# Unread matmuls in idle steps, feed-forward matmuls in halves, and own placing tables for the ends of a chunked recurrence

## The chip, the cores and the metric

The kernel runs on one core of a Trainium2 chip. The metric is the device time of one execution in microseconds (us).

## What is computed

An RWKV-7 block is followed by a routed feed-forward layer. The input is x of 16 sequences, 512 time steps and 128 channels, all in fp32. Cut to what matters:

```
x  = layernorm(layernorm(x)); xn = layernorm(x); dx = shift(xn) - xn
r, k, v, decay, a, g = projections of xn + dx * x_q          # 128x128 and low-rank matmuls
per step: state = state*decay + (state.a)*b + v*k ; o = state.r    # 16 heads of 8x8, 512 steps in sequence
x  = x + (groupnorm(o) + bonus) * g @ W_o
x  = x + square(relu(mix(layernorm(x)) @ W_ffn1)) @ W_ffn2   # 128 -> 512 -> 128
h  = layernorm(x); e = argmax(h @ W_router)                    # 4 experts
y  = x + layernorm(gelu(h @ W1[e] + b1[e]) @ Wo + bo + h)
```

## The kernel before

Channels lie on the 128 partitions and columns are (time step, sequence). The 512 time steps are cut into 16 chunks of 32, so one operation over a chunk has 32 x 16 = 512 columns, which fills one PSUM bank. The recurrence is one chain over all 512 steps, and each step is five instructions: DVE multiplies state by a_t (L824), PE sums over a head (L363, `sa_ps`), DVE makes `upd` (L834), POOL adds the new key-value product to the state (`plus_kv`, L1011), and DVE adds the two (L838). Every second step POOL also makes `s_r` (L1003), and at steps 3, 11, 19 and 27 of a chunk PE sums it into `o_ps` (L356).

All other work of a chunk is hung onto these steps. `pipeline` runs iterations c = -1 to 17 of 32 steps. In iteration c chunk c is scanned, while pieces of chunk c+1 (its projections), of chunk c-1 (group norm, W_o, first feed-forward part) and of chunk c-2 (the experts) are issued. The table `AT` gives each named piece its place, from -32 to 95, counted in steps from the start of the chunk's own scan. Piece p with place n is issued in step n modulo 32. Each engine walks the same loop and, in every step, issues its scan instruction and then the pieces of that step in the order chunk c+1, c, c-1, c-2, within a chunk in the order of the code (`work`). An engine takes its instructions strictly in that order, so a piece that waits holds up the scan instruction of the next step. DVE alone issues pieces between `s_a` and `upd` of the same step, that is, while PE works on the scan sum. Iteration -1 has no scan (the prologue), nor have iterations 16 and 17 (the tail).

Pieces named in the text, with their engine:
- PE: `c0`, `c1`, `gj`, `fc`, `ec`, `wo`, `k`, `v`, `val`, `r`, `g1`, `g2`, `rkb_ps` (one 512-column fp32 matmul each, L314), `wa` (two), `j0`, `j1`, `kks`, `fj`, `ej`, `lj` (sums into 32 rows, L319), `f1` and `f2` (four 512-column matmuls each, L314 and L465), `moe` (16 such, L511, and four bf16 ones for the bias, L514), `mo` (four, L520), `router` (L480), `masks` (16 bf16 transposes, L489), `pick` (L497). An fp32 matmul is two passes (x2 in the rows), each with its own weight load.
- DVE: `bonus`, `best`/`onehot` (the arg max), `h_e` (L962), `xh1` (L852), `cum` (a scan, L871), `kk` (L877), `a_t` (L890), `y1` (L931), `y2` (L969), `lxh` (L973), `res` (L979), `kki` (L886), `kv` (L811, at steps 2, 5, 10, 13, 18, 21, 26, 29).
- ACT: squares (`lsq`), logarithm and exponential for each norm (`rs1`, `frs`, `ers`, `lrs`), `p` (L660, L661), `th_d`, `hid`, `act`, `key`.
- POOL: `k2` (L1025), `x2x` (L1047), `bonus_b` (L1037), `gg` (L1041), `r_t`, `rkb`.
- SP issues all transfers: each norm's row of 1/std is spread over the channels by four transfers (`d_rs1`, `d_frs`, `d_rk`, `d_ers`, `d_lrs`), and `rep` spreads the values for `kv` by eight.

The bank `var_ps` holds only the 128 columns of `fj`; ACT reads them in `frs` and then counts up `fln`.

Of the kernel before, what the change touches and what calls it, by code (L numbers as in the profile page):

```python
# [1102 lines left out]
```

## Time and profile before

| | us |
|---|---|
| three runs: lowest, median, highest | 1220.52, 1222.8, 1224.71 |
| the profiled execution | 1223.49 |
| its span | 1221.7 |
| mean granted TensorE clock, share of full | 0.916 |
| prologue, up to the first `s_a` | 52.7 |
| the 16 scans, to the last `s_a` | 1076.5 |
| tail, from there to the end of the span | 92.5 |
| one scan iteration, from the fifth on | 68 to 68.4 |

The span is the profiled time on the engines; the execution's own time has 1.8 us more around it. The clock column of a window (PEclk) is the granted share of the full TensorE clock of 2.4 GHz, so 0.50 is the level of 1.2 GHz. An engine's idle time costs nothing where it isn't on the chain of the recurrence, so the step, from one `s_a` to the next, is the unit in which this kernel is read.

### The profile page before, as it was taken

Reading aid. Unit: us, or ns where it says so; the run is one execution under the profiler, and the core shown is the slowest. Engines: PE = TensorE matmul, PEld = TensorE weight load, DVE = VectorE, ACT = ScalarE, POOL = GpSimd, SP = SyncE. Lnnn points to the kernel's source line nnn. Section 1 sums busy time; section 2 is a strip of 40 time slices with the busy share of each in tenths; the row PEclk is TensorE's granted clock in tenths of the full one; section 3 lists DMA queues with packets and bytes.
Section 4 is the critical chain, followed back from the end, with each engine's and each line's share of the span. In section 5 each row is a group of like instructions: output and inputs, shape, how many; then the busy total and the mean of one; then the engine's idle time right before and its main releaser. Section 6 shows DMA issues by size and latency. Waiting matters only on the chain.

```text
span 1221.7 us, 16912 instructions
## 1 busy us (share of the span) xinstructions
PE 1023.8 (84%) x4787; PEld 500.2 (41%) x4787; DVE 947.1 (78%) x2283; ACT 604.0 (49%) x965; POOL 675.1 (55%) x885
## 2 busy tenths in 40 slices
...
DMA packets 136485, 75.40 MB, mean 62 GB/s; under 512 B 15292, under 2 KB 129980, under 8 KB 136264
## 3 DMA queue, kind: packets, MB, share of 16 engines
...
q8 instruction: 38, 0.62, 0.2%
...
## 4 chain that ended last, share of the span: by engine, by line
PE 52%; DVE 27%; ACT 10%; issue 7%; DMA 2%; SPq 2%; DVEq 0%; ACTq 0%
PE sa_ps L363 10%; PE fin_a L511 8%; PE fin_b L511 8%; DVE state L838 7%; DVE upd L834 5%; PE pre_a L314 5%; DVE s_a L824 4%; PE fin_b L520 4%; DVE kv L811 3%; PE mid_ps L314 3%; PE o_ps L356 2%; ACT hid L695 2%; PE fin_a L314 2%; ACT hid L697 1%; PE mid_ps L465 1%
## 5 line engine op out<-in xcount | busy, mean ns | idle before, releaser
L1011 POOL TENSOR_TENSOR plus_kv<-state,kv 128x128 f32<-128x128 f32 x512 | 283.7, 554 | 404.7 <-DVE state L838 379.9
L363 PE MATMUL sa_ps<-s_a,con 128*128 128x128 f32 x1024 | 245.0, 323 | 117.6 <-DVE s_a L824 117.3
L363 PEld LDWEIGHTS sa_ps<-s_a,con 128*128 128x128 f32 x1024 | 179.5, 203 | 385.3 <-DVE s_a L824 331.4
L1003 POOL TENSOR_TENSOR s_r<-state,r_t 128x256 f32<-128x256 f32 x256 | 259.6, 1014 | 1.3 <-DVE state L838 1.3
L834 DVE TENSOR_TENSOR upd<-sa_ps,b_t 128x128 f32<-128x128 f32 x512 | 146.8, 287 | 99.4 <-PE sa_ps L363 93.3
L838 DVE TENSOR_TENSOR state<-upd,plus_kv 128x128 f32<-128x128 f32 x512 | 197.7, 386 | 17.5
L824 DVE TENSOR_TENSOR s_a<-state,a_t 128x128 f32<-128x128 f32 x512 | 149.4, 292 | 18.5
L511 PE MATMUL fin_b<-h_e,mat 128*128 128x512 f32 x256 | 133.1, 627 | 1.6 <-ACT pick L710 1.6
L540 ACT ACT_TABLE_LOAD x101 | 129.6, 1283 | 1.8
L811 DVE TENSOR_TENSOR kv<-val_rep,k_t 128x512 f32<-128x512 f32 x128 | 120.2, 940 | 3.0 <-DMA val_rep<-val_c 3.0
L511 PE MATMUL fin_a<-h_e,mat 128*128 128x512 f32 x256 | 122.3, 593 | 0.0
L465 PE MATMUL mid_ps<-hid,mat 128*128 128x512 f32 x128 | 64.2, 605 | 10.0 <-ACT hid L697 10.0
L520 PE MATMUL fin_b<-act,mat 128*128 128x512 f32 x128 | 67.5, 614 | 0.0
L511 PEld LDWEIGHTS fin_a<-h_e,mat 128*128 128x128 f32 x256 | 45.2, 191 | 39.4 <-issue 39.3
L511 PEld LDWEIGHTS fin_b<-h_e,mat 128*128 128x128 f32 x256 | 43.7, 198 | 27.0 <-issue 24.5
L575 ACT ACTIVATE x<-xh_p,vec 128x512 f32<-128x512 f32 x16 | 13.0, 814 | 79.2 <-DVE x L913 63.8
L314 PE MATMUL mid_ps<-z_m,mat 128*128 128x512 f32 x96 | 51.6, 619 | 0.1
L717 ACT ACTIVATE act<-fin_b 128x512 f32<-128x512 f32 x32 | 19.1, 597 | 61.0 <-PE fin_b L514 60.9
L702 ACT ACTIVATE sq_f<-fin_a 128x512 f32<-128x512 f32 x16 | 9.6, 597 | 75.1 <-PE fin_a L314 75.1
L1025 POOL TENSOR_TENSOR k<-key,k 128x512 f32<-128x512 f32 x16 | 27.2, 1699 | 32.7 <-ACT k L630 32.7
L356 PE MATMUL o_ps<-s_r,con 128*32 128x128 f32 x1024 | 42.9, 287 | 0.0
L567 ACT ACTIVATE sq_p<-pre_a 128x512 f32<-128x512 f32 x16 | 9.6, 597 | 67.2 <-PE pre_a L314 67.2
...
## 6 DMA issues: line engine op xcount, KB each, us to landing
val_rep<-val_c SPq DMA_DIRECT2D x512, 64.0 KB, 2.4
rs_p<-row_rs SPq DMA_DIRECT2D x128, 64.0 KB, 2.1
...
```

Of the source, the lines that this page charges most:

```text
L314: return mm(bank_, lhsT, rhs, start=True, stop=True).then_inc(s[name], 1)
L363: mm(sa_ps[:, 0:STATE], k("sum8"), s_a[:], start=True, stop=True).then_inc(s["sa"], 1)
L465: last = mm(mid_ps[:], w("ffn2", j), hid[j][:], start=(j == 0), stop=(j == J - 1))
L511: mm((fin_b, fin_a)[j % 2][:], mat[:, M["W1"] + e * I + j * C:M["W1"] + e * I + (j + 1) * C], h_e[e][:], start=(e == 0), stop=False)
L520: last = mm(fin_b[:], w("Wo", j), act_j[j][:], start=(j == 0), stop=(j == J - 1))
L540: nc.scalar.preload_act_table_set(name)
L811: tt(part, values.rearrange("p (i t b) -> p i t b", i=N // 2, t=QUARTER), keys.unsqueeze(1).broadcast_to([128, N // 2, QUARTER, B]), ALU.m ...
L824: tt(ib(s_a[:]), ib(st(t)), over_i(a_t[c.slot][:, t * B:(t + 1) * B]), ALU.mult).then_inc(s["s_a"], 1)
L834: tt(ib(upd[:]), ib(sa_ps[:, 0:STATE]), over_i(b_t[c.slot][:, t * B:(t + 1) * B]), ALU.mult).then_inc(s["upd"], 1)
L838: tt(st(t + 1), upd[:], plus_kv[:, (t % 2) * STATE:(t % 2 + 1) * STATE], ALU.add).then_inc(s["state"], 1)
L1003: tt(part, states, r.unsqueeze(2).broadcast_to([128, 2, N, B]), ALU.mult).then_inc(s["s_r"], 1)
L1011: tt(plus_kv[:, (t % 2) * STATE:(t % 2 + 1) * STATE], st(t), kv[:, at:at + STATE], ALU.add).then_inc(s["plus_kv"], 1)
```

## The change

- Each chunk takes its places from its own table: `AT_FIRST` for chunks 0 and 1, `AT_LAST` for chunks 14 and 15, `AT` for the others. All three have new places, also for many pieces that are otherwise as before.
- `f1`, `f2`, `moe` and `mo` are issued in halves of 256 columns, each with a place of its own, so these 28 matmuls a chunk become 56. The bias matmul stays whole, behind the second half of the last expert.
- `keep` is new: a matmul of 256 columns of constants (fp32, two passes) into the columns 256 to 511 of `var_ps`, which nothing reads. It waits for the last `fln`, for the bank's sake. There are 11 in `AT`, 20 in `AT_FIRST` and 18 in `AT_LAST`, 12 x 11 + 2 x 20 + 2 x 18 = 208 in all. In `AT` they come in the steps 1 (three), 14, 25, 28, 29, 30 (two) and 31 (two).

No arithmetic that is read is changed.

```diff
 AT = {
-    "c0": -32, "j0": -31, "x_in": -31, "sq0": -30, "rs0": -29, "d_rs0": -24, "xh0": -24, "x1": -24, "c1": -22,
-    "sq1": -22, "j1": -21, "rs1": -20, "d_rs1": -19, "xn": -19, "xh1": -17, "th_w": -17, "key": -17,
-    "wa": -16, "dx": -16, "th_d": -16, "d_rk": -16, "mix_k": -15, "k": -15, "mix_r": -15, "mix_v": -15,
-    "rk": -15, "w2": -14, "val_c": -14, "mix_g": -13, "kks": -12, "v": -11, "val_sb": -11, "k2": -11,
-    "val": -10, "cum": -10, "p": -10, "rep": (-9, 2, 4, 12), "r": -9, "kk": -9, "a_t": -8, "k_t": -7,
-    "r_t": -7, "rec": -6, "rkb": -5, "g1": -4, "kki": -3, "rkb_ps": -3, "b_t": -2, "g2": -2, "th_g": 0,
-    "gate": 0, "bonus": 0, "bonus_b": 13, "x_res": 33, "gsq": 36, "gj": 36, "grs": 36, "gxh": 38, "gaff": 39,
-    "gg": 39, "wo": 40, "x2": 41, "fc": 41, "fsq": 41, "fj": 42, "frs": 43, "xf": 45, "d_frs": 45, "x2x": 47,
-    "fxh": 48, "hid": (51, 51, 55, 61), "kf": 52, "f1": (52, 53, 54, 55), "f2": (56, 57, 57, 58), "d_ers": 58,
-    "y1": 59, "ec": 59, "ej": 59, "esq": 61, "ers": 62, "h": 63, "router": 63, "best": 64, "onehot": 64,
-    "masks": 64, "h_e": (65, 65, 67, 68), "pick": 65, "y1b": 65,
-    "moe": (66, 67, 69, 70, 71, 71, 71, 76, 77, 77, 78, 78, 79, 80, 80, 81), "pick_sb": 66,
-    "act": (71, 76, 76, 79), "mo": (82, 83, 84, 85), "lsq": 84, "y2": 86, "lj": 86, "d_lrs": 89, "lrs": 92,
-    "lxh": 92, "res": 93, "store": 95,
+    "c0": -32, "sq0": -31, "x_in": -31, "j0": -29, "rs0": -29, "x1": -27, "d_rs0": -24, "xh0": -24,
+    "sq1": -23, "d_rs1": -23, "c1": -22, "rs1": -22, "j1": -21, "d_rk": -20, "rep": (-18, 4, 7, 11),
+    "xn": -17, "xh1": -17, "th_w": -17, "key": -16, "wa": -16, "dx": -16, "mix_k": -15, "k": -15,
+    "mix_r": -15, "mix_v": -15, "w2": -14, "th_d": -13, "rk": -13, "mix_g": -13, "kks": -13, "val_c": -12,
+    "v": -11, "cum": -10, "p": -10, "k2": -9, "val": -9, "r": -8, "kk": -8, "val_sb": -8,
+    "keep": (-7, 1, 1, 1, 14, 28, 62, 93, 94, 95, 95), "k_t": -7, "r_t": -7, "rec": -6, "a_t": -5, "rkb": -5,
+    "g1": -4, "rkb_ps": -3, "kki": -3, "th_g": -3, "b_t": -2, "g2": -2, "bonus": 0, "gate": 2, "bonus_b": 3,
+    "x_res": 17, "gsq": 34, "grs": 35, "gj": 36, "fsq": 37, "gxh": 38, "gaff": 39, "gg": 39, "wo": 40,
+    "x2": 41, "fc": 41, "frs": 41, "d_frs": 42, "fj": 42, "x2x": 43, "xf": 47, "fxh": 48,
+    "hid": (51, 52, 57, 60), "kf": 52, "f1": (52, 52, 53, 53, 53, 54, 55, 55),
+    "f2": (56, 56, 57, 57, 58, 58, 58, 58), "d_ers": 57, "y1": 59, "ec": 59, "ej": 59, "esq": 60, "ers": 60,
+    "pick_sb": 63, "h": 63, "router": 63, "best": 64, "onehot": 64, "masks": 64, "h_e": (65, 65, 67, 68),
+    "pick": 65, "y1b": 65,
+    "moe": (66, 66, 66, 67, 68, 69, 69, 69, 70, 70, 70, 70, 71, 71, 71, 71, 72, 74, 75, 75, 75, 76, 76, 76, 77, 77, 77, 78, 79, 80, 81, 81),
+    "act": (67, 68, 76, 80), "mo": (79, 79, 80, 80, 81, 82, 84, 86), "d_lrs": 85, "lsq": 86, "y2": 87,
+    "lj": 87, "lrs": 90, "lxh": 91, "res": 92, "store": 95,
+}
+AT_FIRST = {
...
+    "keep": (-24, -23, -16, -8, -2, -1, 2, 6, 15, 15, 23, 26, 33, 36, 39, 51, 60, 62, 95, 95), "sq1": -24,
...
+    "key": -19, "th_d": -18, "xh1": -17, "wa": -16, "dx": -16, "mix_v": -16, "rk": -15, "mix_k": -15,
+    "k": -15, "mix_r": -15, "w2": -14, "mix_g": -13, "kks": -13, "d_rk": -11, "v": -11, "val": -11, "k2": -11,
...
+    "g2": -2, "gate": -2, "bonus": -1, "bonus_b": 1, "x_res": 28, "gsq": 34, "grs": 35, "gj": 36, "gxh": 38,
...
+}
+AT_LAST = {
...
+    "keep": (-18, -10, -7, -2, 1, 13, 19, 27, 28, 31, 32, 59, 59, 60, 86, 89, 91, 93), "xh1": -17, "key": -16,
...
+    "moe": (68, 68, 68, 69, 69, 70, 70, 71, 71, 71, 71, 72, 73, 74, 74, 74, 74, 76, 76, 77, 77, 78, 78, 78, 79, 79, 79, 81, 82, 83, 84, 84),
...
 }
@@ class Chunk
+        self.place = AT_FIRST if off < 2 else AT_LAST if off >= CHUNKS - 2 else AT
@@ every piece on every engine
-                if at == AT["c0"]:
+                if at == c.place["c0"]:
@@ PE
+            def half(part):
+                return slice(part * COLS // 2, (part + 1) * COLS // 2)
...
                 for j in range(J):
-                    if at == AT["f2"][j]:
-                        pe.wait_ge(s["hid"], c.count(max(j + 1, 3), J))
-                        last = mm(mid_ps[:], w("ffn2", j), hid[j][:], start=(j == 0), stop=(j == J - 1))
-                        if j == J - 1:
-                            last.then_inc(s["f2"], 1)
+                    for part in range(2):
+                        if at == c.place["f2"][2 * j + part]:
+                            pe.wait_ge(s["hid"], c.count(max(j + 1, 3), J))
+                            last = mm(mid_ps[:, half(part)], w("ffn2", j), hid[j][:, half(part)],
+                                      start=(j == 0 and part == 0), stop=(j == J - 1), skip_group_check=True)
+                            if j == J - 1 and part:
+                                last.then_inc(s["f2"], 1)
...
                     sums(fin_b, 0, "mean32", sq_f, "lj")
+                for n in range(len(c.place["keep"])):
+                    if at == c.place["keep"][n]:
+                        if fj_made[0]:
+                            pe.wait_ge(s["fln"], fj_made[0])
+                        mm(var_ps[:, 2 * C:4 * C], k("sum8"), con[:, 0:2 * C], start=True, stop=True, skip_group_check=True)
```

The matmuls of `f1`, `moe` and `mo` are halved in the same way as those of `f2`.

## Rows read from the trace of the kernel before

**Rows 1.** The page, part 1: busy time, share and instructions of each engine.
```profile
PE 1023.8 (84%) x4787; PEld 500.2 (41%) x4787; DVE 947.1 (78%) x2283; ACT 604.0 (49%) x965; POOL 675.1 (55%) x885
```

**Rows 2.** Windows: prologue, iterations 0, 1, 2, 8, first half of the tail.
```profile
core 0: us, PE busy (x) PEld busy (x) DVE busy (x) ACT busy (x) POOL busy (x), PEclk, DMA share, GB/s
0.00:52.70 52.70, 25.57 (x69) 10.43 (x69) 21.71 (x59) 21.66 (x31) 5.59 (x9) 0.81 0.35 96
52.70:117.90 65.20, 38.73 (x162) 20.57 (x162) 48.16 (x120) 20.37 (x30) 37.10 (x50) 0.69 0.34 63
117.90:185.10 67.20, 49.87 (x226) 24.00 (x226) 54.10 (x127) 30.61 (x49) 41.31 (x54) 0.80 0.24 48
185.10:251.90 66.80, 59.07 (x299) 28.28 (x298) 58.49 (x141) 37.36 (x60) 42.44 (x55) 1.00 0.34 68
592.50:660.90 68.40, 61.57 (x299) 30.39 (x299) 58.49 (x141) 37.10 (x60) 42.45 (x55) 0.95 0.33 66
1129.20:1176.80 47.60, 39.89 (x138) 18.14 (x138) 11.50 (x24) 20.18 (x32) 4.94 (x6) 0.85 0.08 22
```

**Rows 3.** The waits: engine, line, waited for: us in total, times, longest us.
```profile
DVE upd L834 <- PE sa_ps L363: 93.3, 167, 1.7
```

**Rows 4.** Windows: around a chunk boundary; single steps; columns as rows 2.
```profile
655.20:658.60 3.40, 1.56 (x5) 0.52 (x4) 3.30 (x8) 0.27 (x2) 1.69 (x2) 1.00 0.65 187
595.10:598.40 3.30, 3.20 (x31) 2.40 (x29) 2.09 (x6) 0.66 (x2) 1.23 (x2) 0.68 0.64 103
187.60:189.70 2.10, 1.64 (x25) 1.09 (x22) 2.00 (x6) 0.34 (x2) 1.23 (x2) 1.00 0.44 72
614.70:616.20 1.50, 1.29 (x30) 0.89 (x26) 0.85 (x4) 1.48 (x3) 0.56 (x1) 1.00 0.02 5
59.94:61.77 1.83, 0.79 (x2) 0.50 (x2) 0.88 (x3) 0.00 (x0) 1.24 (x2) 0.50 0.56 101
```

**Rows 5.** Timeline of DVE at a chunk boundary: start us, us, what, idle before.
```profile
596.52 1.29 DVE L962 TENSOR_TENSOR h_e<-fin_b,h 128x512 f32<-128x512 bf16 x2 [1.14 <-PE fin_b L489]
```

**Rows 6.** Timeline of DVE and POOL in step 7 of iteration 8.
```profile
608.14 1.26 POOL L1041 TENSOR_TENSOR z_m<-z_m,gate 128x512 f32<-128x512 f32 x1 [0.63 <-DVE z_m L908]
608.29 1.25 DVE L838 TENSOR_TENSOR state<-upd,plus_kv 128x128 f32<-128x128 f32 x1
```

**Rows 7.** Windows: steps 11-15, 18-19, 21-24, 27-29 of iteration 8.
```profile
614.70:623.30 8.60, 8.14 (x52) 4.07 (x48) 5.97 (x17) 5.72 (x11) 6.49 (x9) 1.00 0.23 52
628.80:633.00 4.20, 4.20 (x30) 2.00 (x29) 3.50 (x8) 3.65 (x6) 2.25 (x3) 1.00 0.00 0
634.90:644.60 9.70, 9.01 (x34) 4.17 (x32) 7.97 (x18) 8.02 (x15) 6.59 (x7) 1.00 0.43 68
649.00:656.80 7.80, 5.17 (x36) 2.17 (x36) 6.71 (x15) 3.15 (x5) 4.05 (x6) 1.00 0.15 35
```

**Rows 8.** Timeline of DVE, iteration 8: waits for a DMA and for PE.
```profile
621.93 0.69 DVE L852 TENSOR_TENSOR xh_p<-pre_a,rs_p 128x512 f32<-128x512 f32 x1 [0.46 <-DMA rs_p<-row_rs]
...
636.71 0.29 DVE L834 TENSOR_TENSOR upd<-sa_ps,b_t 128x128 f32<-128x128 f32 x1 [0.61 <-PE sa_ps L363]
```

**Rows 9.** Timeline of POOL, iteration 8: an operation that moves.
```profile
635.51 1.71 POOL L1025 TENSOR_TENSOR k<-key,k 128x512 f32<-128x512 f32 x1
```

**Rows 10.** Timeline of ACT, iteration 8: an exponential of the next chunk.
```profile
641.37 1.11 ACT L660 ACTIVATE p_all<-cum_bt 128x512 f32<-128x512 f32 x1
```

**Rows 11.** Timeline of PE, iteration 8: matmuls with different weights back to back.
```profile
637.37 1.02 PE L314 MATMUL fin_a<-z_m,mat 128*128 128x512 f32 x2
638.23 1.02 PE L520 MATMUL fin_b<-act,mat 128*128 128x512 f32 x2
```

**Rows 12.** The chain of waits at the end: start us, us, what.
```profile
1137.21 2.05 PE fin_b L511 x2
...
1188.59 6.62 PE fin_b L511 x8
...
1195.43 3.44 PE fin_a L511 x8
```

More of the change, by code:

```diff
@@ new lines @@
+    "act": (67, 68, 76, 80), "mo": (79, 79, 80, 80, 81, 82, 84, 86), "d_lrs": 85, "lsq": 86, "y2": 87,
+    "lj": 87, "lrs": 90, "lxh": 91, "res": 92, "store": 95,
+}
+AT_FIRST = {
[4 rows of a table added]
+    "k": -15, "mix_r": -15, "w2": -14, "mix_g": -13, "kks": -13, "d_rk": -11, "v": -11, "val": -11, "k2": -11,
+    "val_c": -10, "cum": -10, "r": -10, "val_sb": -9, "rep": (-9, 4, 5, 11), "kk": -8, "r_t": -8, "a_t": -8,
+    "p": -7, "k_t": -7, "rkb": -6, "g1": -6, "rec": -6, "rkb_ps": -5, "kki": -5, "b_t": -4, "th_g": -3,
+    "g2": -2, "gate": -2, "bonus": -1, "bonus_b": 1, "x_res": 28, "gsq": 34, "grs": 35, "gj": 36, "gxh": 38,
[3 rows of a table added]
+    "pick_sb": 61, "h": 63, "router": 63, "y1b": 63, "best": 64, "onehot": 64, "masks": 64,
+    "h_e": (65, 65, 67, 68), "pick": 65,
+    "moe": (66, 66, 66, 67, 68, 69, 69, 69, 70, 70, 70, 70, 70, 71, 71, 71, 74, 75, 75, 75, 76, 76, 77, 77, 78, 79, 79, 80, 80, 80, 81, 81),
+    "act": (67, 69, 76, 81), "mo": (78, 79, 81, 82, 82, 86, 86, 86), "d_lrs": 80, "y2": 87, "lj": 87,
+    "lsq": 87, "lrs": 90, "lxh": 92, "res": 92, "store": 92,
+}
@@ new lines @@
+AT_LAST = {
+    "c0": -32, "x_in": -32, "sq0": -31, "j0": -29, "rs0": -29, "x1": -28, "d_rs0": -24, "sq1": -24,
+    "xh0": -24, "d_rs1": -23, "c1": -22, "rs1": -21, "j1": -21, "d_rk": -20, "xn": -19, "th_w": -18,
+    "keep": (-18, -10, -7, -2, 1, 13, 19, 27, 28, 31, 32, 59, 59, 60, 86, 89, 91, 93), "xh1": -17, "key": -16,
+    "wa": -16, "dx": -16, "th_d": -15, "mix_k": -15, "k": -15, "mix_r": -15, "mix_v": -15, "rk": -15,
+    "w2": -14, "val_c": -14, "mix_g": -13, "v": -13, "kks": -12, "p": -12, "cum": -11, "rep": (-11, 1, 3, 11),
+    "k2": -9, "val": -9, "val_sb": -9, "r": -8, "kk": -8, "k_t": -7, "r_t": -7, "rec": -6, "a_t": -5,
+    "rkb": -5, "g1": -4, "rkb_ps": -4, "kki": -3, "g2": -3, "th_g": -2, "b_t": -2, "gate": -2, "bonus": 0,
+    "bonus_b": 13, "gsq": 34, "grs": 35, "gj": 36, "x_res": 38, "gxh": 39, "fsq": 39, "gaff": 40, "gg": 40,
[3 rows of a table added]
+    "best": 63, "onehot": 63, "y1b": 64, "esq": 64, "masks": 64, "ers": 65, "pick_sb": 66,
+    "h_e": (66, 66, 68, 69), "pick": 67,
+    "moe": (68, 68, 68, 69, 69, 70, 70, 71, 71, 71, 71, 72, 73, 74, 74, 74, 74, 76, 76, 77, 77, 78, 78, 78, 79, 79, 79, 81, 82, 83, 84, 84),
+    "act": (68, 72, 75, 83), "d_lrs": 80, "mo": (82, 83, 83, 83, 84, 84, 85, 86), "lj": 87, "lsq": 87,
+    "lrs": 88, "y2": 89, "lxh": 91, "res": 92, "store": 93,
@@ L412, in work @@
                     one(pre_a[:], val_scan[:], mix["v"][:], "v")
-                if at == AT["kks"]:
+                if at == c.place["kks"]:
                     pe.wait_ge(s["sqk"], c.count())
@@ L482, in work @@
                     last.then_inc(s["router"], 1)
-                if at == AT["masks"]:
+                if at == c.place["masks"]:
                     pe.wait_ge(s["onehot"], c.count(3, 3))
@@ L493, in work @@
                             last.then_inc(s["masks"], 1)
-                if at == AT["pick"]:
+                if at == c.place["pick"]:
                     pe.wait_ge(s["h_e"], c.count(2, E))
```

238 lines of the change are left out of this document (123 added, 115 removed), and 8 rows, old and new, of tables (AT_FIRST, AT_LAST).

## The prediction

> **What bounds the kernel now.** I read part 1 of the page first: PE is busy 84% and DVE 78% of the span, so neither is full, and no busy share tells what a change is worth [rows 1]. The windows by iteration come next: the scans take 1076.5 of 1221.7 us, an iteration 68.4 us in the steady part, which is 2.14 us a step [rows 2]. Single steps say what that is made of. Step 11 of iteration 8, in which DVE has only its three scan instructions, takes 1.5 us; that is the chain itself, and 32 of it would be 49 us [rows 4]. The other 19 us are steps in which something stands in the chain's way, and there are four kinds.
>
> First, the clock. In iteration 2 it is 1.00 throughout; in iteration 8 it is 0.95 [rows 2]. In the stretch before the chunk boundary PE is busy 1.56 of 3.40 us, and in step 1 behind it the clock is at 0.68, part at 1.2 GHz [rows 4]. That step takes 3.3 us, where its twin at 2.4 GHz takes 2.1, because DVE waits 1.14 us for the 16 transposes of `masks` [rows 4, 5]. The falls come once in a chunk. Second, PE: it holds up `upd` 93.3 us in 167 steps [rows 3], as in step 21, by 0.61 us [rows 8]. Third, transfers: `xh1` waits 0.46 us for its row [rows 8]. Fourth, POOL: in step 7 the state addition takes 1.25 us, where the scan's other instructions take 0.29 [rows 8], and ends 0.14 us after POOL's `gg`, with which it overlaps [rows 6]. I take from this that a POOL piece holds the state to its own end plus 0.15.
>
> **The change, per steady iteration (4 to 12, nine of them; all pieces from the new `AT`).** Stretches are those of iteration 8.
>
> - *Clock.* Seven of the eleven `keep` come in steps 25 and 28 to 31, three in step 1, one in step 14. One is 256 columns in two passes, half of a 512-column matmul, of which two stand 0.86 us apart at 2.4 GHz [rows 11]; so 0.43 us. Six are in steps 28 to 31, and three of them, 1.3 us, in the very stretch in which PE was busy 1.56 of 3.40 [rows 4], which makes it 2.85. I take it that the clock then stays up: step 1 takes 2.1 for 3.3, **-1.2**. The `keep` cost nothing as long as PE would idle: those of steps 28 to 30 end before the next scan sum's input, those of step 31 make the sum of step 0 about 0.6 us late, but `upd` of that step waits for `bonus` and the arg max on DVE anyway, and those of step 1 stand before `pick`, which waits for `h_e` (1.29 us [rows 5]). Without that cover it is 11 x 0.43 = 4.7 us an iteration.
> - *Steps 11 to 15 (8.6 us [rows 7]).* `x2x` comes from step 15 to 11: it starts 0.6 us into the step behind `plus_kv`, lasts as long as `gg`, 1.26 [rows 6], so step 11 becomes 2.05, +0.5. Three `moe` halves follow there on 1.29 us of PE work [rows 4]; 2.6 us from the sum's start at 0.35 are 3.0 to 3.15 with the changes of tile, against an input ready at 2.4, so step 12 has its sum 0.75 late, +0.75. `bonus_b` leaves step 13, -0.2. In step 15 the wait of 0.46 [rows 8] is covered by the longer steps before it, and `x2x` is gone, -0.65. **+0.4**. Steps 3 and 4 take `bonus_b` and stay in sum.
> - *Steps 8 and 16.* Four halves of `moe` stand before the sum of step 8 in place of three whole ones, and `fxh` no longer waits for its row: **-0.3**, bounded by 0 and 0.5.
> - *Steps 18 and 19 (4.2 us, PE busy throughout [rows 7]).* One half of `mo` is there for four: 1.3 us less of PE, of which 0.5 stood before `upd`, half of it won since `kks` comes to step 19: **-0.25**.
> - *Steps 21 to 24 (9.7 us [rows 7]).* Step 21: `kv` alone, 1.7, its 0.61 on PE [rows 8] hidden; step 22: `cum` alone, 2.4; step 23: `y2`, but `k2` (1.71 [rows 9]) now comes here, 0.6 + 1.7 + 0.15 = 2.45. At its end PE stands at `lj`, which waits for `lsq`; in ACT's new order the two exponentials of `p`, 1.11 each [rows 10], come before it, so `lj` is done about 1.1 us after the next sum's input, and the step 24 takes 2.7. 9.3 in all: **-0.4**. Queued behind `lj` is the scan sum, and on it DVE. If ACT is early this is -1.4, if it is 1 us later +0.6.
> - *Steps 25, 27 to 29, 31.* Step 25 +0.1, since `rec` and so `r_t` is later. Steps 27 to 29 were 7.8 [rows 7]: step 27 now carries `a_t`, `y1` and `lxh`, 3.2; 28 `res`, 1.9; 29 `kv` and `kki`, 2.4; 7.5, -0.3. Step 31 -0.1. **-0.3**.
>
> Sum: -1.2 + 0.4 - 0.3 - 0.25 - 0.4 - 0.3 = **-2.05**, so 66.3 us.
>
> *Halves.* Each needs two more weight loads. In the rows a 128x128 fp32 load with other weights lies between any two passes, and these stay 0.43 us apart [rows 11]; a half's pass lasts 0.21. I cost the loads at nothing; the bounds are 0 and 0.11 each (a load has 128 columns, a quarter of a 0.43 pass). The Trainium skill (TensorE: Matmul & The Clock Gate, Part 3, The mechanism) says that a weight load overlaps a running matmul only where its row group differs, which is never so here. By that rule 56 loads an iteration would be added to PE. Rows 11 show the loads hidden on the same row groups.
>
> **Outside the steady part.** Iterations 3, 13 and 14 mix tables: -1.5 each, -4.5. Iteration 15: -1.5. Iterations 0 to 2 take 65.2, 67.2 and 66.8 us [rows 2]; a bare step at 1.2 GHz takes 1.83 for 1.5 [rows 4], 0.3 more; so with the clock held up, 20 of them in iteration 0 would win 6. The clock is low there because PE has little to do, and 12 `keep` (5 us of 65) are few; I take -3 for the three, bounds +4 and -12. Prologue (52.7): a `keep` stands between `wa` and `k` on the chain, 0.86 at 1.2 GHz, and `bonus` (0.68) now comes before the first `s_a`: +1.5. Tail (92.5): PE is at 1.2 GHz from 1126 to 1143; a pair of passes of 0.86 takes 2.05 there [rows 12]. `keep` in steps 27 to 31 of iteration 15 should hold it, and `gj` comes ahead of the first `moe`: -6, bounds 0 and -9. The last `moe` bank (6.62 for 3.44 [rows 12]) follows a transfer during which no `keep` can run; nothing won.
>
> Sum: 9 x 2.05 = 18.5, + 4.5 + 1.5 + 3 + 6 - 1.5 = 32. The profiled execution took 1223.5, 0.7 above the median of 1222.8, so I predict **1191 us**.
>
> **Rivals.**
> 1. *PE was the whole of it.* The halves take away nearly all of the 93.3 us [rows 3], and my delays in steps 12 and 24 don't come. 1.75 us more in nine iterations, and first iterations at their bound: 1191 - 16 - 4 = 1171. For it: in 167 steps PE ends last. Against: once PE is early, DVE's pieces or POOL's are next, as in steps 21 and 7. 0.17.
> 2. *The clock falls all the same.* Then 12 x 1.2 and 4 in the tail come back: 1209. For it: the Trainium skill (same page, Part 4) says that transposes don't count as PE work, and 16 stand at the boundary; no row here separates that. Against: PE's busy time there goes from 1.56 to 2.85 of 3.40. 0.08.
> 3. *The gain is eaten*, most likely by `lj` and the full queue of ACT in steps 22 to 25, 2.3 us an iteration in 13, 30 us: 1221. 0.06.
> 4. *Slower: the `keep` stand in the scan's way.* PE is in order, and the scan sum waits behind them. All 208 uncovered would be 89 us; from 36% of them on (32 us) the change loses; with half, 1191 + 44 = 1235. Against: the steps chosen are those in which PE idles. 0.05.
> 5. *Slower: the weight loads of the halves aren't hidden.* 56 x 16 loads of 0.11 are 99 us; a half of it on the chain gives 1240. Rows 11 speak against it; the page's rule above is this rival. 0.02.
>
> My forecast has 0.62. The range of 8 in 10 reaches from rival 1 to rival 2, **1170 to 1210**. Faster by over 0.3% (3.7 us, about what a measurement of this kernel can tell from none): 0.62 + 0.17 + 0.08 = 0.87. Of rival 3's 0.06, 0.05 is no change and 0.01 slower; with rivals 4 and 5 slower has 0.08.
>
> **What would show it.** Right: PEclk 1.00 in every window from iteration 3 to 14; step 1 at 2.1 us with no wait of `h_e` over 0.2; iteration 8 at 66.3; `upd` waiting for PE in step 12 and in step 24, there behind `lj`; a long state addition in steps 3, 11 and 23; PE in the first half of the tail at full clock. Wrong: windows at 0.50 at the boundary (rival 2); scan sums whose wait ends behind a `keep` (rival 4); passes of a half over 0.25 us apart (rival 5); an iteration over 68 us, or under 65 (rival 1).

## The result, and the profile after

The changed kernel takes **1195.18 us** (median of four runs, 1193.75 to 1197.01) against 1223.61 for the kernel before beside it. The ratio is 0.9772, with an interval of 0.9749 to 0.9796. I had predicted 1191 us, and 1170 to 1210 as the range: the sign is right, and the time was 4 us too fast. The profiled execution took 1195.53 us, with a span of 1193.7. Executions that were disturbed are left out of every number below; one of the runs, a_more, was profiled in such an execution, so no row of it is shown.

The page, part 1, and the clock line of part 2 (each digit is the granted clock of a fortieth of the span, in tenths), against [rows 1]:

```profile
PE 1054.8 (88%) x6099; PEld 713.3 (60%) x6099; DVE 940.2 (79%) x2283; ACT 605.3 (51%) x965; POOL 650.4 (54%) x885
...
PEclk9769899999999999999999999999999999999989
```

The windows that answer to [rows 2]: prologue, iterations 0, 1, 2, 8 and 15, first half of the tail. Columns are start:end and length in us, busy time (instructions) of PE, PEld, DVE, ACT and POOL, the clock, the transfers' share and GB/s.

```profile
0.00:53.40 53.40, 28.42 (x81) 13.46 (x81) 22.19 (x61) 21.67 (x31) 5.01 (x9) 0.84 0.35 92
53.40:118.60 65.20, 43.25 (x186) 24.27 (x186) 48.63 (x121) 20.82 (x30) 36.66 (x51) 0.76 0.34 64
118.60:184.90 66.30, 50.97 (x268) 29.92 (x268) 51.80 (x125) 30.33 (x48) 40.59 (x55) 0.90 0.25 50
184.90:252.80 67.90, 63.06 (x381) 43.56 (x381) 58.22 (x141) 37.25 (x60) 40.82 (x55) 1.00 0.34 67
584.00:650.50 66.50, 62.48 (x377) 42.63 (x378) 58.23 (x140) 37.20 (x60) 40.83 (x55) 1.00 0.34 69
1048.30:1109.70 61.40, 51.47 (x322) 36.84 (x321) 42.63 (x121) 21.25 (x33) 34.56 (x52) 1.00 0.23 44
1109.70:1152.00 42.30, 39.42 (x216) 29.71 (x216) 11.27 (x24) 20.03 (x32) 5.18 (x6) 1.00 0.09 23
```

Iteration 8 takes 66.5 us for 68.4, and its clock is 1.00 for 0.95. From 151.5 to 1155 us no window of the trace is at half clock, where the kernel before had one fall at every chunk boundary from iteration 3 on. Iterations 0 to 2 took 199.4 us where they had taken 199.2: nothing was won there. The last iteration is longer than before, 61.4 for 58.9. The tail, from the last `s_a` at 1109.7 on, is 84.1 us for 92.5.

The waits of DVE, against [rows 3]:

```profile
DVE upd L894 <- PE sa_ps L405: 80.7, 118, 1.7
...
DVE kv L871 <- DMA val_rep<-val_c: 23.3, 28, 3.2
```

DVE waits 12.6 us less for PE. Instead there is a wait that the prediction didn't have: `kv` waits for the spread values, 23.3 us in all.

The windows of steps that answer to [rows 4] and [rows 7] (steps 11 to 15, 18 to 19, 21 to 24, 26, 27 to 29, and step 1 of iteration 8; the last one is the stretch of 3.4 us ahead of the next boundary):

```profile
604.90:613.87 8.97, 8.80 (x71) 7.15 (x64) 6.11 (x18) 5.52 (x10) 5.39 (x8) 1.00 0.24 54
619.24:623.48 4.24, 3.93 (x31) 2.15 (x30) 3.12 (x8) 3.39 (x5) 1.80 (x3) 1.00 0.11 19
625.40:633.95 8.55, 8.06 (x40) 5.09 (x39) 7.68 (x16) 8.41 (x14) 6.15 (x7) 1.00 0.36 58
636.42:638.82 2.40, 2.32 (x12) 1.66 (x10) 1.52 (x5) 0.08 (x1) 1.24 (x2) 1.00 0.73 188
638.82:646.52 7.70, 6.18 (x41) 2.93 (x40) 7.50 (x16) 3.15 (x5) 4.49 (x5) 1.00 0.17 38
...
586.58:588.63 2.05, 2.05 (x21) 1.82 (x18) 1.98 (x6) 0.00 (x0) 1.23 (x2) 1.00 0.63 107
...
647.10:650.50 3.40, 3.08 (x18) 2.26 (x18) 3.04 (x8) 0.00 (x0) 1.71 (x3) 1.00 0.75 222
```

Step 1 takes 2.05 us for 3.3, and PE is busy 3.08 of the 3.4 us ahead of the boundary, where it had been busy 1.56.

### The profile page after: what moved, and what is told of

Its sections match the earlier page's. It is cut to its first block, busy times and chain, and to the rows that moved or that the text cites. A ratio compares the mean times of both kernels' runs of the same rounds, so it can differ in the third digit from the quotient of the medians.

```text
span 1193.7 us, 19599 instructions
## 1 busy us (share of the span) xinstructions
PE 1054.8 (88%) x6099; PEld 713.3 (60%) x6099; DVE 940.2 (79%) x2283; ACT 605.3 (51%) x965; POOL 650.4 (54%) x885
## 4 chain that ended last, share of the span: by engine, by line
PE 36%; DVE 20%; SPq 19%; issue 10%; ACT 8%; DMA 6%; POOL 0%; DVEq 0%; ACTq 0%; POOLq 0%
SPq L314 10%; SPq L301 6%; PE fin_b L564 6%; PE fin_a L564 5%; DMA val_rep<-val_c 5%; PE sa_ps L405 5%; DVE state L898 4%; PE mid_ps L356 4%; PE pre_a L356 3%; DVE upd L894 3%; PE var_ps L586 3%; ACT L600 3%; SPq L298 3%; DVE kv L871 2%; DVE s_a L884 1%
## 5 line engine op out<-in xcount | busy, mean ns | idle before, releaser
L898 DVE TENSOR_TENSOR state<-upd,plus_kv 128x128 f32<-128x128 f32 x512 | 191.8, 375 | 17.6
L884 DVE TENSOR_TENSOR s_a<-state,a_t 128x128 f32<-128x128 f32 x512 | 149.4, 292 | 18.5
L564 PE MATMUL fin_b<-h_e,mat 128*128 128x256 f32 x512 | 136.9, 394 | 4.0 <-ACT pick L770 4.0
L871 DVE TENSOR_TENSOR kv<-val_rep,k_t 128x512 f32<-128x512 f32 x128 | 117.8, 921 | 23.9 <-DMA val_rep<-val_c 23.3
L564 PE MATMUL fin_a<-h_e,mat 128*128 128x256 f32 x512 | 127.9, 379 | 0.0
L586 PE MATMUL var_ps<-con 128*128 128x256 f32 x416 | 120.7, 400 | 0.0
L564 PEld LDWEIGHTS fin_b<-h_e,mat 128*128 128x128 f32 x512 | 91.6, 192 | 35.9 <-issue 23.9
L564 PEld LDWEIGHTS fin_a<-h_e,mat 128*128 128x128 f32 x512 | 93.1, 190 | 22.8 <-issue 13.4
L586 PEld LDWEIGHTS var_ps<-con 128*128 128x128 f32 x416 | 75.4, 200 | 30.3 <-issue 26.3
L574 PE MATMUL fin_b<-act,mat 128*128 128x256 f32 x256 | 71.4, 385 | 0.0
L515 PE MATMUL mid_ps<-hid,mat 128*128 128x256 f32 x256 | 64.6, 385 | 0.0
L574 PEld LDWEIGHTS fin_b<-act,mat 128*128 128x128 f32 x256 | 47.4, 190 | 17.4 <-ACT act L777 10.1
L515 PEld LDWEIGHTS mid_ps<-hid,mat 128*128 128x128 f32 x256 | 46.3, 190 | 14.9 <-ACT hid L757 9.9
```

The lines of the kernel that those rows point to most:

```text
L564: mm(to[:, half(part)], mat[:, M["W1"] + e * I + j * C:M["W1"] + e * I + (j + 1) * C], h_e[e][:, half(part)], start=(e == 0 and part == 0) ...
L574: last = mm(fin_b[:, half(part)], w("Wo", j), act_j[j][:, half(part)], start=(j == 0 and part == 0), stop=(j == J - 1), skip_group_check=True)
L586: mm(var_ps[:, 2 * C:4 * C], k("sum8"), con[:, 0:2 * C], start=True, stop=True, skip_group_check=True)
L871: tt(part, values.rearrange("p (i t b) -> p i t b", i=N // 2, t=QUARTER), keys.unsqueeze(1).broadcast_to([128, N // 2, QUARTER, B]), ALU.m ...
L884: tt(ib(s_a[:]), ib(st(t)), over_i(a_t[c.slot][:, t * B:(t + 1) * B]), ALU.mult).then_inc(s["s_a"], 1)
L898: tt(st(t + 1), upd[:], plus_kv[:, (t % 2) * STATE:(t % 2 + 1) * STATE], ALU.add).then_inc(s["state"], 1)
```

## The experiments

Twelve kernels were run, all with the whole computation. Where an edit needs a table written anew, the line numbers of its profile are other than those of the changed kernel; the names of tiles are the same. Step lengths below are medians over iterations 3 to 13 of the profiled execution, from one `s_a` to the next.

### The parts, each taken away or tried alone

```diff
a_nokeep
-    "keep": (-7, 1, 1, 1, 14, 28, 62, 93, 94, 95, 95), ...
+    "keep": (), ...                       # in all three tables
```

> The changed kernel with all keep lists empty; halves, places and tables as they are. Theory (the keep hold the clock, and that is 1.2 us of step 1 in each of 12 or 13 iterations and some 4 to 8 us of the tail): one window at half clock returns in every chunk, step 1 takes 3.3 us again, the kernel takes 1195 + 15 + 5 = about 1215 us, at least 1208. Rival (the clock would hold without them, by the new places of the halves, and the keep only stand in the way): 1195 or less, step 1 at 2.1 us. Rival (the gain is mostly the clock, the rest of the change is worth nothing): 1224.

Measured: 1214.3 us (ten runs, 1208.6 to 1220.0), ratio 0.9926 (0.9901 to 0.9950); 19.1 us more than with `keep`. Step 1 is at 3.10 us again, the tail at 86.6. The windows of step 0 and step 1 of iteration 9:

```profile
660.70:663.30 2.60, 2.23 (x6) 1.06 (x7) 2.35 (x12) 0.00 (x0) 1.25 (x2) 0.64 0.63 102
663.30:666.60 3.30, 2.66 (x23) 1.98 (x21) 2.08 (x6) 0.08 (x1) 1.23 (x2) 0.77 0.63 102
```

The clock falls at this boundary without them and doesn't with them. Of the thirteen boundaries ahead of iterations 3 to 15, all have such a fall in the kernel before, ten in a_nokeep (not those of 4, 8 and 11) and none in the changed kernel. So the `keep` do hold it, and of the first rival (it would have held by the new places) only these three boundaries are left.

```diff
b_keep, against the kernel before
 AT = {
+    "keep": (-7, 1, 1, 1, 14, 28, 62, 93, 94, 95, 95), ...
@@ TensorE, at the end of work(c, at)
+                for n in range(len(AT["keep"])): ...      # as in the change
```

> The kernel before with nothing new but the eleven keep matmuls, at the changed kernel's places for the middle chunks, in every chunk. Theory: the clock stays up from about iteration 2 on, step 1 goes from 3.3 to 2.1 us, 12 or 13 x 1.2 = 15 us, the tail wins some 4 us more: about 1204 us. Rival (the keep cost time where the old order has PE on the chain: 93 us of waits of upd for PE): 1210 or more, with upd <- PE above 93 us although the clock is up.

Measured: 1213.9 us, ratio 0.9919 (0.9889 to 0.9949), 9 us won for the 19 expected. Step 1 is at 2.05 us, so the clock's 1.2 us came in full. What is lost lies elsewhere: step 15 takes 2.59 us for 2.16 and step 3 takes 1.73 for 1.53. In step 14 of iteration 9 the `keep` stands ahead of two `moe` matmuls, 1.88 us together, and the next scan sum behind them; the waits show it as well:

```profile
DVE upd L930 <- PE sa_ps L450: 107.8, 211, 2.4
...
687.58 0.60 PE L622 MATMUL var_ps<-con 128*128 128x256 f32 x2
...
688.02 1.88 PE L601 MATMUL fin_b<-h_e,mat 128*128 128x512 f32 x4
...
689.95 0.38 PE L450 MATMUL sa_ps<-s_a,con 128*128 128x128 f32 x2
```

So a `keep` costs by what stands behind it in PE's queue: of the 1.2 us that step 1 wins here, steps 3 and 15 give back 0.6. Set beside the 19 us of the changed kernel, though, the 9 us are no clean comparison, since there the first and last chunks have 20 and 18 `keep` for eleven. By the profiled executions `keep` wins 21.6 us there (from a_nokeep to the changed kernel) and 6.4 here; in iterations 4 to 12 that is 8.0 and 6.1, so most of the gap lies outside the steady part. Iterations 0 to 2 alone win 2.4 us there and lose 1.8 here.

```diff
b_halves: the changed code with the old table
-    "f1": (52, 53, 54, 55), "moe": (66, 67, 69, ...), ...
+    "f1": (52, 52, 53, 53, 54, 54, 55, 55), "moe": (66, 66, 67, 67, 69, 69, ...), ..., "keep": ()
```

> The kernel before with each feed-forward matmul issued as two halves one behind the other at the old place, no keep, old places. It prices the halving alone. Theory (the two additional weight loads of each pair are hidden behind passes, also behind the shorter ones of 0.21 us): 1223 us within 2 us, PE busy unchanged. Rival (a load is only hidden where the row group differs, 56 x 16 x 0.11 us = 99 us of PE): over 1235 us, and the two passes of a half stand over 0.25 us apart.

Measured: 1223.6 us, ratio 1.0012 (0.9997 to 1.0028). An iteration is 68.1 us. In iteration 8, a whole matmul of 512 columns (`c1`) and two halves of `moe` at one place, and the group, by form, of the weight loads of such halves (count | busy us, mean ns | idle before):

```profile
613.23 1.02 PE L611 MATMUL pre_a<-x,con 128*128 128x512 f32 x2
...
616.67 1.03 PE L819 MATMUL fin_a<-h_e,mat 128*128 128x256 f32 x4
...
L819 PEld LDWEIGHTS fin_b<-h_e,mat 128*128 128x128 f32 x32 | 5.6, 190 | 0.7 <-issue 0.2
```

The four passes of the halves take 1.03 us from the first's start to the last's end, the two passes of the whole one 1.02, although there are four weight loads for two. The loads are hidden. Halving costs nothing that can be measured, and by itself it wins nothing.

```diff
a_whole
-    "moe": (66, 66, 66, 67, 68, 69, ...), "mo": (79, 79, 80, 80, 81, 82, 84, 86), ...
+    "moe": (66, 66, 68, ...), "mo": (79, 80, 81, 84), ...      # place of the first half
-    mm(to[:, half(part)], ..., h_e[e][:, half(part)], start=(e == 0 and part == 0), ...)
+    mm(to[:], ..., h_e[e][:], start=(e == 0), ...)              # and so f1, f2, mo
```

> The changed kernel with whole matmuls at the place where it has the first half of each; keep and all other places stay. Theory (the halves were only worth what PE no longer delays: a half more in front of a scan sum is 0.43 us where the two halves lay in different steps): 3 to 6 pairs an iteration are split over two steps, some of them behind waits; 0.5 to 1 us an iteration more, 1203 to 1211 us. Rival (halving is worth nothing, the order of the places is): 1195 within 2 us.

Measured: 1212.8 us, ratio 0.9928 (0.9905 to 0.9951), 17.6 us more than with halves, a little over the top of what I expected. An iteration is 67.5 us for 66.2, and DVE waits for PE longer than in the kernel before:

```profile
DVE upd L1149 <- PE sa_ps L660: 109.8, 179, 3.4
```

The difference lies in the steps in which a second half now stands ahead of a scan sum: step 3 2.03 for 1.60, step 9 1.94 for 1.52, step 12 2.42 for 2.15, steps 21 and 22 +0.31 and +0.40. Steps 5 and 14 take 0.25 and 0.22 more. Steps 24 and 26 are shorter by 0.37 and 0.48.

```diff
a_places: a_whole with
+    "keep": ()                                             # in all three tables
```

> The changed kernel without any keep and with whole feed-forward matmuls at the place of the first half: only the new places of the three tables are left of the change. It completes the square: places alone, with keep (1212.8), with halves (1214.3), with both (1195.2). Theory (keep and halves are each worth about 18 us on the new places and don't depend on one another): 1212.8 + 1214.3 - 1195.2 = 1232 us, so the new places alone are slower than the kernel before. Rival (they overlap, each wins most of what the other would): 1216 to 1223 us.

Measured: 1231.6 us, ratio 1.0060 (1.0038 to 1.0082). The expectation was 1232, from adding the two losses. So with the medians of the runs the square is

| us | no `keep` | `keep` |
|---|---|---|
| old places, whole | 1223 | 1213.9 |
| old places, halves | 1223.6 | not run |
| new places, whole | 1231.6 | 1212.8 |
| new places, halves | 1214.3 | 1195.2 |

On the new places `keep` wins 19 us with or without halves (18.8 and 19.1), and halves win 17 to 18 us with or without `keep` (17.3 and 17.6). These four values are medians of single groups of runs; from the ratios, each against the kernel before of its own group, either part comes to some 16 us without the other and 19 with it, with about 4 us to either side. The new places alone lose 8.6 us: the steady iteration stays at 68.1, the tail takes 86.5 us for 92.5, but iteration 0 takes 70.7 us for 65.2 and iteration 15 takes 65.5 for 58.9. In iterations 4 to 12 of the profiled executions the mean is 68.2 us before, 68.3 in a_places, 67.8 in a_whole, 67.2 in a_nokeep and 66.4 in the changed kernel. On the old places `keep` is worth 9 us, with eleven in every chunk, and halving nothing.

```diff
a_one
-        self.place = AT_FIRST if off < 2 else AT_LAST if off >= CHUNKS - 2 else AT
+        self.place = AT                                    # by giving all three tables AT's places
```

> The changed kernel with the middle table for all sixteen chunks. It prices the two additional tables. Theory (my sums: they win little at the start, since iterations 0 to 2 took 199.4 us against 199.2, and in the tail the keep hold the clock, 6 us): 1195 + 3 to + 8, so 1198 to 1203 us, the tail 87 to 92 us for 84. Rival (the tables are what the first iterations live on, by twenty keep in the first two chunks): over 1206 us, with more windows at half clock in iterations 0 to 2. Rival (they are worth nothing or hurt, as by x2 in the last iteration): 1195 or less.

Measured: 1203.5 us, ratio 0.9847 (0.9832 to 0.9861), 8.3 more than with the three tables. By the profiled executions (1202.2 and 1193.7): the tail is 90.5 us for 84.1, the last iteration 56.3 for 61.4, iterations 0 and 1 are equal within 0.4, and iterations 2 to 14 are 6.8 us longer, 5.6 of it in iterations 4 to 12, whose instructions are the same in both. The table for the end so wins 6.4 in the tail and gives 5.1 back in the last iteration. The 6.8 us are told of in the section on transfers.

### The price of `keep`

```diff
a_keep7
-    "keep": (-7, 1, 1, 1, 14, 28, 62, 93, 94, 95, 95), ...
+    "keep": (-7, 28, 62, 93, 94, 95, 95), ...                # AT alone
```

> The changed kernel whose middle table has seven keep for eleven: the three in step 1 and the one in step 14 are left out, those in steps 25 and 28 to 31 stay. Theory (the boundary is the only idle place, and three of them in the stretch ahead of it carry the clock): clock 1.00 as before, 1195 us within 2. Rival (the three of step 1 are needed): a window at half clock behind the boundary in some or all chunks, steps 2 to 4 some 0.5 to 1.2 us longer, 1200 to 1210 us. Rival (those of step 1 stood ahead of pick and cost time): 1192 or less.

Measured: 1200.4 us, ratio 0.9821 (0.9802 to 0.9839): 5 us more, where I expected none. The clock is a part of it: it fell once, from 761.7 to 765.1 us, and step 21 of that iteration takes 3.33 us for 1.76. By medians step 3 is 0.08 us shorter and step 26 0.48, but step 18 takes 3.04 us for 2.41. The rest is transfers; see below.

```diff
a_keep2
-    "keep": (-7, 1, 1, 1, 14, 28, 62, ...), ...
+    "keep": (-7, -7, 1, 1, 1, 1, 1, 1, 14, 14, 28, 28, 62, 62, ...), ...      # AT alone
```

> The changed kernel with each of the eleven keep of the middle table issued twice, 4.7 us more of PE an iteration, 57 us in twelve iterations. It prices what cover the keep have. Theory (those of steps 28 to 30 end before the scan sum's input comes, those of step 1 stand in front of pick, which waits for h_e for 1.29 us that three of them already fill; the one in step 14 delays): 1 us an iteration more, 1207 us. Rival (all cover is used up): 1195 + 57 = 1252 us. Rival (all of it is idle time): 1195 within 2.

Measured: 1227.8 us, ratio 1.0041 (1.0021 to 1.0061): 33 us for 57 us of matmuls, about midway between my value and the rival. Steps 28 to 30 and step 15 are as before (1.92, 2.38, 1.92, 1.52): there PE idles and a second `keep` is free. All the cost is at the boundary: step 31 +0.86, step 1 +0.36, step 2 +0.70, step 3 +0.65. The windows of the steps 31 and 1 to 2, in which PE has no idle time left in the first two:

```profile
659.70:662.50 2.80, 2.80 (x19) 2.59 (x19) 1.86 (x5) 0.00 (x0) 0.56 (x1) 1.00 0.67 169
665.10:667.50 2.40, 2.40 (x26) 2.25 (x24) 2.06 (x6) 0.00 (x0) 1.23 (x2) 1.00 0.36 58
667.50:670.10 2.60, 2.10 (x14) 1.71 (x13) 1.72 (x5) 0.94 (x2) 1.69 (x2) 1.00 0.62 101
```

So the eleven of the change stand just at the edge of their cover.

### The new wait: transfers in SP's queue

In the changed kernel, iteration 8, DVE and SP's queue around step 18 (SP's time is that of issuing, us; x8 are eight issues):

```profile
610.70 2.72 SPq L301 DMA_DIRECT2D rs_m<-row_frs  x4
613.53 5.11 SPq L314 DMA_DIRECT2D val_rep<-val_c  x8
620.51 0.69 DVE L871 TENSOR_TENSOR kv<-val_rep,k_t 128x512 f32<-128x512 f32 x1 [0.98 <-DMA val_rep<-val_c]
```

An issue takes SP 0.60 us, so the eight of `rep` take 4.8, and they now begin only behind the eight of `d_rs1` and `d_frs`, which wait for rows that ACT has to finish. In iteration 8 of the kernel before, `rep` went first and SP had issued it by 610.2 us, 19 us ahead of its `kv`. The prediction speaks of the rows for `xh1` and `fxh`, and not of `rep`.

```diff
a_rep3
-    "rep": (-18, 4, 7, 11), ...
+    "rep": (-18, 4, 7, 8), ...                  # 8 for 11 in all three tables
```

> The changed kernel with the fourth replication of the values (rep, quarter 3) three places earlier in SP's queue, behind d_rs0 and ahead of d_rs1 and d_frs, as in the kernel before. It is for the new wait in the trace: in step 18 kv waits 0.98 us for val_rep. Theory (the wait is due to the queue order): kv's wait in step 18 goes, the step goes from 2.41 to 1.93 us, 0.5 x 12 = 6 us, 1189 us. Rival (the place only moves the wait: d_rs1 and d_frs are issued up to 4.8 us later, so xh1 or fxh in step 15 waits for its row as in the kernel before, 0.6 us): 1195 us within 2.

Measured: 1195.9 us, ratio 0.9774 (0.9750 to 0.9797), the four runs at 1190.6, 1195.8, 1195.9 and 1197.3. The profiled one is that of 1190.6. In it step 18 is at 2.00 us and step 19 at 1.91 for 1.72, `kv` waits 10.0 us in all for 23.3, and the iteration is 65.8 us as the sum of medians, 65.3 in iterations 10 to 12. So the wait was due to the order. The total shows no gain, for two reasons. One is visible in a_best below. The other I can't show: the other three runs had a mean clock of 0.960 to 0.964 for 0.973, and only one was profiled.

How late the values come varies also with something else. In a_keep7, iteration 9, the same eight issues take 6.17 us, and in the changed kernel's iteration 9 they take 5.07:

```profile
683.02 6.17 SPq L399 DMA_DIRECT2D val_rep<-val_c  x8
...
691.06 0.69 DVE L956 TENSOR_TENSOR kv<-val_rep,k_t 128x512 f32<-128x512 f32 x1 [1.82 <-DMA val_rep<-val_c]
```

```profile
679.74 5.07 SPq L314 DMA_DIRECT2D val_rep<-val_c  x8
```

One of the eight took 1.1 us longer, and `kv` waits 1.82 us for 0.98. Such long issues are spread over every run: in the changed kernel 25 of SP's 950 issues took 0.9 to 2.0 us where the median is 0.60. The group over iteration 8 has one of 1497 ns (minimum, median and maximum in ns):

```profile
L314 SPq DMA_DIRECT2D val_rep<-val_c x34: 548/600/1497, 583.7 to 650.7; - x34
```

Here they fall on steps 0 to 3 and 22 to 25 in most iterations. At the first place one iteration, 12, shows a waiter (`kv` in step 2, 2.49 us for 1.92). The second delays `rep` of quarter 0, for which step 26 waits (2.40 us for 1.92; [0.81] in iteration 8). In iterations 6 to 12 of a_keep7 no long issue falls there, and step 26 takes 1.92 us.

In a_keep7 they fall on `d_frs` and on step 25 in iterations 3 to 5, and on steps 16 and 17, on `rep` of quarter 3, from iteration 6 to 12. Iterations 3 to 6 are 3.7 us longer than in the changed kernel, by steps 15, 16 and 26. In iterations 7 to 13 step 18 takes 3.0 to 3.4 us, 5.7 more in all, step 26 wins 3.2 of that back, the fall of the clock costs 1.6, and the sum is 3.2 more. In iteration 13 no issue is long and step 18 still takes 3.02 us, as the values land 2.6 us after their last issue for 1.8.

In a_one they fall on steps 16 and 17 in iterations 2 to 5, where step 18 takes 2.9 to 3.4 us, 3.2 more in all. Step 21 is 1.5 us longer in iterations 4 and 5, and that is the clock: it is at half from 360.9 to 364.3 and from 429.2 to 432.6 us, just these steps. Iterations 6 to 9 are 3.2 us longer, with long issues on steps 12 to 15 and 25. What makes an issue long no run here isolates.

### The last iteration, and a version with both repairs

In the changed kernel, iteration 15, step 8 takes 5.42 us for 1.65. `x2` of chunk 14 stands one place earlier in `AT_LAST` than anywhere else, so DVE comes to it before its input exists, with `upd` behind it:

```profile
1064.79 1.26 POOL L1101 TENSOR_TENSOR z_m<-z_m,gate 128x512 f32<-128x512 f32 x1
1066.10 0.30 PEld L356 LDWEIGHTS mid_ps<-z_m,mat 128*128 128x128 f32 x2 [1.72 <-POOL z_m L1101]
...
1067.27 0.69 DVE L973 TENSOR_TENSOR x<-mid_ps,x 128x512 f32<-128x512 f32 x1 [3.02 <-PE mid_ps L356]
```

```diff
a_x2
-    "x2": 40, ...                                          # AT_LAST
+    "x2": 41, ...
```

> The changed kernel with x2 of the last two chunks one step later (41 for 40), where the kernel before has it. In step 8 of the last iteration DVE stands at x2 with the scan's product already there, since x2 waits for gate x state on POOL and the projection on PE, 3.02 us; the step takes 5.42 us where the kernel before has 1.65. Theory: step 8 falls to about 1.7, step 9 rises by at most 1, so 2.7 to 3.7 us less: 1192 us. Rival (what follows, fc and the tail's own chain, is bound by x2's input and not by the scan): no change, 1195.

Measured: 1194.8 us, ratio 0.9772 (0.9753 to 0.9792). The difference of 0.4 us is within what can be told. In the profiled execution step 8 is at 3.14 us and step 9 at 2.34 for 1.52, so of the 3.8 us 1.5 are won there. Steps 22 and 23 take 1.7 more, in which the clock is at half (1090.2 to 1093.6 us); a_best below has the same steps 8 and 9 without such a fall, and an iteration 15 that is 1.5 us shorter. Step 8 doesn't get to 1.7, since the state addition waits for POOL's `gg` to end:

```profile
1065.16 1.25 POOL L1186 TENSOR_TENSOR z_m<-z_m,gate 128x512 f32<-128x512 f32 x1
1065.30 1.26 DVE L983 TENSOR_TENSOR state<-upd,plus_kv 128x128 f32<-128x128 f32 x1
```

```diff
a_more: a_rep3 and a_x2, and
-    "keep": (-7, 1, 1, 1, 14, ...), ...
+    "keep": (-13, -7, -5, -5, 1, 1, 1, 14, ...), ...         # AT, and the same three in AT_LAST
```

> The changed kernel with rep of quarter 3 behind d_rs0 (as in the run a_rep3), x2 of the last two chunks at 41 (as in a_x2), and three keep more in an iteration, two in step 27 and one in step 19, in which PE has idle time. Theory (in a_rep3 the profiled run took 1190.6 us at a mean clock of 0.973, the three others 1195.8 to 1197.3 at 0.960 to 0.964: the transfer's wait is gone in all of them, but the clock falls in some; more keep hold it): 1189 us, clock 0.972 or more in all runs. Rival (the three keep cost more than they hold, or the falls have another place): 1195 or more.

Measured: 1202.7 us, ratio 0.9814 (0.9786 to 0.9842), mean clock 0.961 to 0.968. Against a_best below, which lacks only the three `keep`, that is 8.8 us more, and the mean clock is no higher (0.962 to 0.971 there): the rival. Without a row I can't say in which step.

```diff
a_best: a_rep3 and a_x2 together
```

> The changed kernel with the two repairs together and no more keep: rep of quarter 3 behind d_rs0 (as in a_rep3) and x2 of the last two chunks at 41 (as in a_x2). Theory (both win what their steps show, 0.4 us in twelve iterations and 1 us once, and the windows at half clock that a_rep3 showed in three of its four runs come by the phase of an iteration): 1189 to 1195 us, the mean clock of the faster runs near 0.973 and of the slower ones near 0.962; steps 18 at 2.0 us in either. Rival (the queue order wins nothing; the one run at 1190.6 was chance): 1195 within 1, and step 18 at 2.0 with another step as much longer.

Measured: 1193.9 us (1191.5 to 1195.8), ratio 0.9757 (0.9737 to 0.9777). It is ahead of the changed kernel by 1.3 us, which its interval doesn't separate from it. In iterations 4 to 14 it is 4.2 us ahead (725.2 us for 729.4), in iterations 0 to 2 it is 5.1 us behind, and 4.4 us of that are one step. I had moved `rep` in the first chunks' table too, and there it comes to stand ahead of `d_rs0`, whose row is ready first:

```profile
58.76 10.06 SPq L569 DMA_DIRECT2D val_rep<-val_c  x10
68.92 2.51 SPq L556 DMA_DIRECT2D rs_p<-row_rs  x4
72.98 0.69 DVE L1161 TENSOR_TENSOR xh_p<-pre_a,rs_p 128x512 f32<-128x512 f32 x1 [4.72 <-DMA rs_p<-row_rs]
```

a_rep3 has the same step, at 6.25 us. With the old place in `AT_FIRST` a_best would come to an estimated 1189.5 us (1193.9 - 4.4). It wasn't tried.

## Why the prediction was right, by its own steps

**Clock, -1.2: right.** Step 1 went from 3.28 to 2.05 us, and no window between iterations 3 and 14 is at half clock. The busy time ahead of the boundary is 3.08 of 3.40 for my 2.85. a_nokeep takes it back at ten of thirteen boundaries. Rival 2 is out, and with it the reading of the Trainium skill (TensorE: Matmul & The Clock Gate, Part 4) that could have made the fall come anyway; that the 16 transposes don't count as PE work no run here shows or refutes, as the clock held in their presence.

**Steps 11 to 15, +0.4: +0.3 measured.** Step 11 is 2.02 us (2.05 predicted), step 12 2.15 (2.3), step 13 1.73 (0.2 less than 1.88 predicted), steps 14 and 15 1.52 each.

**Steps 8 and 16, -0.3: -0.2.** 1.52 for 1.65 and 2.32 for 2.40.

**Steps 18 and 19, -0.25: -0.1, from two misses.** Step 19 went to 1.72, where the sum had 2.05. Step 18 went to 2.41 for 1.92: the wait for `val_rep`, which is the first thing the prediction didn't have.

**Steps 21 to 24, -0.4: -1.1.** The mechanisms are there, the sizes are not. `k2` takes 1.28 us where I priced it with the 1.71 of [rows 9], and the state addition ends 0.14 us after it, as [rows 6] had it, so step 23 is 2.03 for 2.45. `lj` does stand in the way behind the exponentials, with `upd` waiting for the sum, but the sum starts 0.9 us after its input (the end of `s_a`), not 1.1, and step 24 is 2.36 for 2.7. In iteration 8:

```profile
630.13 1.28 POOL L1085 TENSOR_TENSOR k<-key,k 128x512 f32<-128x512 f32 x1
...
630.76 0.79 DVE L898 TENSOR_TENSOR state<-upd,plus_kv 128x128 f32<-128x128 f32 x1
...
631.59 0.29 DVE L884 TENSOR_TENSOR s_a<-state,a_t 128x128 f32<-128x128 f32 x1
...
631.74 0.63 ACT L781 ACTIVATE sq_f<-y 128x512 f32<-128x512 f32 x1
...
632.42 0.43 PE L361 MATMUL fin_b<-sq_f,con 128*32 128x128 f32 x8 [0.30 <-ACT sq_f L781]
632.77 0.49 PE L405 MATMUL sa_ps<-s_a,con 128*128 128x128 f32 x2
...
633.30 0.29 DVE L894 TENSOR_TENSOR upd<-sa_ps,b_t 128x128 f32<-128x128 f32 x1 [0.56 <-PE sa_ps L405]
```

**Steps 25, 27 to 29, 31, -0.3: -0.3.** Step 27 is 3.39 (3.2), 28 1.92 (1.9), 29 2.38 (2.4), together 7.7 as before and not 0.3 less. Step 31 won 0.28 for 0.1, and b_halves has it at 1.92 us too, without `keep` or new places. So the sum here is right by luck. And step 26, which I had not listed, took 0.48 more by the second wait for `val_rep`.

By medians the sum is -2.1 us for a predicted -2.05, 66.2 us for 66.3; as a mean over iterations 4 to 12 it is 66.4 us. It is a hit by luck in part, since 1.0 us of unforeseen waits (steps 18 and 26) stands against 1.1 us in steps 19, 23 and 24 that I had priced too high.

**Halves at nothing: right.** b_halves gives 1.0012. The Trainium skill's rule (TensorE: Matmul & The Clock Gate, Part 3, The mechanism), that a load overlaps a running matmul only where the row group differs, would have made 99 us by the prediction's estimate, and the trace speaks against it. The same section also names a background weight buffer as an exception, which the prediction left out; the loads are hidden, and by what no run here shows. That halving, at nothing in itself, is worth 17.6 us on the new places by letting one half stand ahead of a scan sum and the other behind it, my sum holds only step by step; I never had it as a number.

**`keep` cover: right, and thin.** Iteration 8 has its 11, 4.7 us, and no step with a `keep` is longer than predicted. With whole matmuls the three of step 1 aren't covered: step 3 takes 2.03 us in a_whole and 1.62 in a_places. a_keep2 shows that a second set would cost 58% of its time. Rival 4 had the mechanism right, and b_keep shows it at work in steps 3 and 15 of the old order.

**Outside the steady part: two of five wrong, the others right within 2.4 us.** Iterations 0 to 2: -3 predicted, +0.2 measured. The step that failed is that I saw only the `keep` there: a_places has 205.7 us, a_nokeep 201.7 and a_whole 198.9 against 199.4 and the 199.2 of before. So the new places took 6.5 us, which I had put at nothing, and `keep` won 6.7 without halves and 2.4 with them. Iterations 3, 13 and 14: -1.9 and -4.4 for -4.5, a miss of 1.7. Iteration 15: -1.5 predicted, +2.5 measured. Step 8 is 3.8 us longer by `x2`, whose place in `AT_LAST` I had not compared with that in `AT`; a_x2 gets back 1.5 of them. Step 27 is 2.3 us longer, and no run is about it. Tail: -8.4 for -6, within the bounds, but by another split than mine. a_places and a_nokeep, without any `keep`, have tails of 86.5 and 86.6 us for the 92.5 of before, so the new places give 5.9 us and `keep` 2.5. With the places of `AT` in a_one it is 90.5. The clock is 1.00 up to 1155 us, and the bank that begins at 1161.65, at half clock for part of it, takes 5.46 us against 6.62 [rows 12], where I had seen nothing won. Prologue: +0.7 for +1.5.

The two banks in the chain that ended last, the first of them partly at half clock:

```profile
1161.65 5.46 PE fin_b L564 x16
1167.33 3.46 PE fin_a L564 x16
```

Altogether iterations 4 to 12 won 16.7 us for 18.5, iterations 3, 13 and 14 won 6.2 for 4.5, the start nothing for 3, the last iteration lost 2.5 for a gain of 1.5, the prologue lost 0.7 for 1.5, and the tail won 8.4 for 6: 28 us for 32. The step of the prediction that failed is the sum outside the steady part: it has iterations 0 to 2 as a gain by `keep` alone and iteration 15 as a gain, and no price for the new places in either.
